# The first stage's projection as three fp32r passes, with statistics a quarter ahead, two load buffers and the normalisation on ScalarE

## The reference

```
x = x + ssm(layernorm(x))      # depthwise conv of 4 taps, projection 512 -> 48, a scan over 2048 steps, 16 -> 512
x = x + moe(layernorm(x))      # router over 64 experts, top 8, expert FFNs 512 -> 256 -> 512, and a shared expert
```

## Time and profile before

| what | value |
|---|---|
| median of 3 runs | 3797.72 us (3794.5 to 3801.96) |
| the profiled execution | 3804.61 us |
| its span | 3802.9 us |
| TensorE busy over the span | 3527.6 us, 93% |
| VectorE, ScalarE, GpSimd busy | 2331.9, 1363.0, 1736.2 us |
| granted TensorE clock over the span | 0.972 of full |
| `ssm_inputs`, TensorE's first transpose to its last matmul | 31.52 to 197.9 us |

### The profile page before, as it was taken

How to read it: one execution, slowest core, us unless ns; L and a number is a source line. 1 busy time by engine, 2 the same in 40 slices (tenths; PEclk the granted TensorE clock), 3 DMA queues, 4 the chain that set the end, 5 groups by cost and what they waited for, 6 DMA issues and landing times.

```text
span 3802.9 us, 109938 instructions
## 1 busy us (share of the span) xinstructions
PE 3527.6 (93%) x17240; PEld 2860.7 (75%) x17241; DVE 2331.9 (61%) x5877; ACT 1363.0 (36%) x4103; POOL 1736.2 (46%) x1372
## 2 busy tenths in 40 slices
PE   5929999589999999999999999999999999999995
PEld 3518888378787888787888788888887878888884
DVE  5457888555656666566555656665565666656552
ACT  2224444133334333343333433333333334333331
POOL 1011212145555555555555555555555555555543
PEclk9969999789999999999999999999999999999998
DMA  3323333256767666676667666666666677667654
GB/s 126 105 80 124 119 128 115 52 130 122 159 141 166 148 135 140 142 172 139 140 111 159 157 131 123 142 142 142 127 140 125 139 174 157 139 127 170 128 99 72
DMA packets 217551, 502.59 MB, mean 132 GB/s; under 512 B 47504, under 2 KB 47632, under 8 KB 217114
## 3 DMA queue, kind: packets, MB, share of 16 engines
q0 software_dynamic: 129024, 320.94, 45.4%
q1 hardware_dynamic: 87130, 176.22, 13.8%
q10 hardware_dynamic: 1344, 4.85, 0.4%
HBM read 1115.79 MB, written 191.41 MB: 344 GB/s over the span
## 4 chain that ended last, share of the span: by engine, by line
PE 73%; issue 3%; DMA 2%; DVE 1%; DVEq 1%; ACT 1%; ACTq 0%; POOLq 0%; POOL 0%; SPq 0%
PE e_ps_gu L1597 41%; PE e_ps_y L1616 20%; PE e_ps_x L1567 7%; PE e_ps_h L1626 3%; DMA out<-e_y,e_y_ids 2%; PE e_ps_find L1579 1%; DVE e_w_low L1738 1%; DVEq L1451 0%; ACT e_w_high L1675 0%; DVE e_below L1781 0%; ACT e_xT_high L1683 0%; DVEq L1741 0%; ACTq L1451 0%; DVE e_xT_low L1746 0%; DVEq L1738 0%
## 5 line engine op out<-in xcount | busy, mean ns | idle before, releaser
L1531 POOL DMA_INDIRECT out<-e_y,e_y_ids x576 | 992.7, 1723 | 1237.1 <-SPq L1501 600.9
L1597 PE MATMUL e_ps_gu<-e_w_high,e_xT_high 128*128 x2304 | 687.6, 419 | 32.8 <-issue 27.3
L1523 POOL DMA_INDIRECT e_x<-token_rows,e_x_ids x576 | 618.4, 1074 | 214.3 <-issue 169.9
L1597 PE MATMUL e_ps_gu<-e_w_high,e_xT_low 128*128 x2304 | 636.7, 398 | 0.0
L1597 PE MATMUL e_ps_gu<-e_w_low,e_xT_high 128*128 x2304 | 635.2, 398 | 0.0
L1694 ACT ACTIVATE e_silu<-e_ps_gu 128x256 f32<-128x256 f32 x576 | 221.3, 384 | 1018.1 <-PE e_ps_gu L1597 839.4
L1765 DVE TENSOR_SCALAR e_y<-e_ps_y,e_weight 128x512 f32 (+1 forms) x576 | 430.4, 747 | 235.9 <-PE e_ps_y L1616 196.8
L1746 DVE TENSOR_TENSOR e_xT_low<-e_ps_x,e_xT_high 128x512 fp32r<-128x512 f32 x576 | 397.5, 690 | 269.6 <-ACT e_xT_high L1683 123.0
L1597 PEld LDWEIGHTS e_ps_gu<-e_w_high,e_xT_low 128*128 128x128 f32 x2304 | 436.4, 189 | 107.3
L1597 PEld LDWEIGHTS e_ps_gu<-e_w_low,e_xT_high 128*128 128x128 f32 x2304 | 434.6, 189 | 102.4
L1597 PEld LDWEIGHTS e_ps_gu<-e_w_high,e_xT_high 128*128 128x128 f32 x2304 | 396.0, 191 | 113.2 <-issue 51.1
(11 more groups left out here) (292 smaller groups left out, 4141.5 us busy)
## 6 DMA issues: line engine op xcount, KB each, us to landing
e_w_raw<-in_L_ffn_we_gate SPq DMA_DIRECT2D x576, 512.0 KB
e_w_raw<-in_L_ffn_we_up SPq DMA_DIRECT2D x576, 512.0 KB
e_w_raw<-in_L_ffn_we_down SPq DMA_DIRECT2D x576, 512.0 KB
a_x<-in_L_attn_x SPq DMA_DIRECT2D x64, 256.0 KB, 3.6
t_x_in<-in_L_attn_x SPq DMA_DIRECT2D x64, 256.0 KB, 2.7
token_rows<-t_xn SPq DMA_DIRECT2D x64, 256.0 KB, 2.0
out<-t_y_out SPq DMA_DIRECT2D x64, 256.0 KB, 2.0
e_x<-token_rows,e_x_ids POOLq DMA_INDIRECT x576
```

The lines of the kernel that those rows point to most:

```text
L1523: pool.indirect_dma_start(x[:, s % XS, :], None, k.rows, bass.IndirectOffsetOnAxis(x_ids[:, s:s + 1], 0)) \
L1531: pool.indirect_dma_start(k.out, bass.IndirectOffsetOnAxis(y_ids[:, s:s + 1], 0), y[:, s % YS, :], None, compute_op=ALU.add).then_inc(adde ...
L1597: last = nc.tensor.matmul(ps_gu[s % 2][:], x[:, s % 2, c, :], w[:, c], start=(n == 0), stop=(n == 3 * DC - 1))
```

## The change

- The product becomes three passes in fp32r: `a_wtap_high` and `a_wtap_low` are made once; the turned block is kept as `a_xT_high` (ScalarE, `keep_high`) and `a_xT_low` (VectorE, `keep_low`: turned minus high). A quarter's product is 24 matmuls of 128x512 in place of 8 fp32 ones.
- TensorE's order: the product of quarter n - 1 is cut in four parts of six matmuls, and one part follows each transposed block of quarter n.
- VectorE takes the statistics of quarter n + 1 before the subtractions of quarter n, and computes `a_shift` = -mean * rstd behind them. It no longer normalises.
- ScalarE normalises (`normalize`: x * rstd + shift), a block ahead of the high copies. The stores of a batch (`store`) follow the batch's last product, which is now finished in the next batch's first quarter.
- `a_x` has two buffers of four blocks. `a_xT_low` lies in memory (`shared_rows`) that `scan_states` later uses for the states and the output weights.

```diff
-        x_in = sb("a_x", [P, SUB, D])
+        x_in = sb("a_x", [P, 2, SUB, D])
         stats = sb("a_stats", [P, SUB, 6])
         moments = sb("a_moments", [P, SUB, 2])
         var_eps = sb("a_var_eps", [P, SUB])
-        rstd = sb("a_rstd", [P, SUB])
+        rstd = sb("a_rstd", [P, 2, SUB])
+        shift = sb("a_shift", [P, 2, SUB])
         xn = sb("a_xn", [P, SUB, D])
-        xnT = sb("a_xnT", [P, DC, L + 2])
+        xT_high = sb("a_xT_high", [P, DC, L + 2], F32R)
+        xT_low = k.shared_rows[:].rearrange("p (c l) -> p c l", c=DC)
...
+        wtap_high = sb("a_wtap_high", [P, 2, DC, P], F32R)
+        wtap_low = sb("a_wtap_low", [P, 2, DC, P], F32R)
...
-                        sp.wait_ge(normed, NT * b + SUB * q + s + 1)
-                        sp.dma_start(x_in[:, s, :], k.x_blocks[b, SUB * q + s]).then_inc(x_loaded[s], 16)
+                        after(sp, normed, SUB * (n - 2) + s + 1)
+                        sp.dma_start(x_in[:, q % 2, s, :], k.x_blocks[b, SUB * q + s]).then_inc(x_loaded[q % 2][s], 16)
...
+            nc.vector.tensor_copy(wtap_high[:], wtap[:])
+            v.drain()
+            nc.vector.tensor_tensor(wtap_low[:], wtap[:], wtap_high[:].bitcast(F32), ALU.subtract)
             v.drain().then_inc(w_ready, 1)
+            def spread(b, q):
+                half, load = q % 2, 2 * b + q // 2
+                for s in range(SUB):
+                    v.wait_ge(x_loaded[half][s], 16 * load + 16)
+                    nc.vector.bn_stats(stats[:, s, :], x_in[:, half, s, :])
+                v.drain()
+                for s in range(SUB):
+                    nc.vector.bn_aggr(moments[:, s, :], stats[:, s, :])
+                v.drain()
+                nc.vector.tensor_scalar(var_eps[:], moments[:, :, 1], LN_EPS, None, ALU.add).then_inc(var_ready, 1)
+
+            def shifts(b, q):
+                v.wait_ge(rstd_ready, QT * b + q + 1)
+                nc.vector.scalar_tensor_tensor(out=shift[:, q % 2], in0=moments[:, :, 0], scalar=-1.0,
+                                               in1=rstd[:, q % 2], op0=ALU.mult, op1=ALU.mult).then_inc(shift_ready, 1)
+
+            def keep_low(b, q, s):
+                i = SUB * (QT * b + q) + s
+                v.wait_ge(xT_high_ready, i + 1)
+                after(v, product_done, QT * b + min(q + 2, QT) - QT)
+                at = 1 + P * (SUB * q + s)
+                nc.vector.tensor_tensor(xT_low[:, :, at:at + P], turned[s][:], xT_high[:, :, at:at + P].bitcast(F32),
+                                        ALU.subtract).then_inc(xT_low_ready, 1)
+
+            def batch(b):
+                for q in range(QT):
+                    next_b, next_q = (b, q + 1) if q + 1 < QT else (b + 1, 0)
+                    more = not isinstance(next_b, int) or next_b < B
+                    if more:
+                        spread(next_b, next_q)
+                    for s in range(SUB):
+                        keep_low(b, q, s)
+                    if more:
+                        shifts(next_b, next_q)
+
+            spread(0, 0)
+            shifts(0, 0)
             v.wait_ge(bias_summed, 1)
             nc.vector.tensor_tensor(bias[0:PROJ, :], bias_ps[0:PROJ, :], b48[:], ALU.add).then_inc(bias_ready, 1)
-
-            with v.Fori(0, B * QT) as n:
-                for s in range(SUB):
-                    v.wait_ge(x_loaded[s], 16 * n + 16)
-                    nc.vector.bn_stats(stats[:, s, :], x_in[:, s, :])
-                v.drain()
-                for s in range(SUB):
-                    nc.vector.bn_aggr(moments[:, s, :], stats[:, s, :])
-                v.drain()
-                nc.vector.tensor_scalar(var_eps[:], moments[:, :, 1], LN_EPS, None, ALU.add).then_inc(var_ready, 1)
-                v.wait_ge(rstd_ready, n + 1)
-                for s in range(SUB):
-                    v.wait_ge(turned_done, SUB * n + s + 1)
-                    nc.vector.tensor_scalar(xn[:, s, :], x_in[:, s, :], moments[:, s, 0:1], rstd[:, s:s + 1],
-                                            ALU.subtract, ALU.mult).then_inc(normed, 1)
+            peeled(v, B, batch)
...
+            def turn(b, q, s):
+                i = SUB * (QT * b + q) + s
+                pe.wait_ge(normed, i + 1)
+                after(pe, xT_low_ready, i + 1 - SUB)
+                for c in range(DC):
+                    last = nc.tensor.transpose(turned[s][:, c, :], xn[:, s, c * P:(c + 1) * P], k.ident[:])
+                last.then_inc(turned_done, 1)
+
+            def project(b, q, part):
+                n = QT * b + q
+                pair, first = part // 2, 6 * (part % 2)
+                if part == 0:
+                    pe.wait_ge(xT_low_ready, SUB * (n + 1))
+                    after(pe, proj_ready, n - 1)
+                if part == 2 and q + 1 < QT:
+                    pe.wait_ge(xT_low_ready, SUB * (n + 1) + 1)
+                at = QL * q + 2 * pair
+                passes = [(x, w, c) for x, w in ((xT_high, wtap_high), (xT_high, wtap_low), (xT_low, wtap_high))
+                          for c in range(DC)]
+                for j in range(first, first + 6):
+                    x, w, c = passes[j]
+                    last = nc.tensor.matmul(product[q % 2][:], w[:, pair, c, :], x[:, c, at:at + QL],
+                                            start=(part == 0 and j == 0), stop=(part == 3 and j == 11))
+                if part == 3:
+                    last.then_inc(product_done, 1)
+
+            def batch(b):
+                for q in range(QT):
+                    last_b, last_q = (b, q - 1) if q > 0 else (b - 1, QT - 1)
+                    for s in range(SUB):
+                        turn(b, q, s)
+                        if not isinstance(last_b, int) or last_b >= 0:
+                            project(last_b, last_q, s)
+
+            peeled(pe, B, batch)
+            for part in range(4):
+                project(B - 1, QT - 1, part)
...
+            def normalize(b, q, s):
+                n = QT * b + q
+                if s == 0:
+                    act.wait_ge(shift_ready, n + 1)
+                after(act, turned_done, SUB * (n - 1) + s + 1)
+                nc.scalar.activation(xn[:, s, :], x_in[:, q % 2, s, :], ACT.Identity, bias=shift[:, q % 2, s:s + 1],
+                                     scale=rstd[:, q % 2, s:s + 1]).then_inc(normed, 1)
+
+            def keep_high(b, q, s):
+                act.wait_ge(turned_done, SUB * (QT * b + q) + s + 1)
+                after(act, product_done, QT * b + min(q + 2, QT) - QT)
+                at = 1 + P * (SUB * q + s)
+                nc.scalar.copy(xT_high[:, :, at:at + P], turned[s][:]).then_inc(xT_high_ready, 1)
...
-                act.wait_ge(product_done, QT * b + q + 1 + QT)
+                act.wait_ge(product_done, QT * b + q + 1)
...
+            def store(b):
                 nc.scalar.copy(proj[0:PROJ, L - 1:L], b48[:]).then_inc(last_set, 1)
...
+            def batch(b):
+                for q in range(QT):
+                    normalize(b, q, 0)
+                    for s in range(1, SUB):
+                        normalize(b, q, s)
+                        keep_high(b, q, s - 1)
+                    keep_high(b, q, SUB - 1)
+                    if q > 0:
+                        keep_product(b, q - 1)
+                    elif not isinstance(b, int) or b > 0:
+                        keep_product(b - 1, QT - 1)
+                        store(b - 1)
+
             peeled(act, B, batch)
+            keep_product(B - 1, QT - 1)
+            store(B - 1)
...
-            k.wout_high = sb("wout_high", [P, B, D], F32R)
-            k.wout_low = sb("wout_low", [P, B, D], F32R)
-            k.states = sb("states", [P, 2, L], F32R)
+            k.shared_rows = sb("shared_rows", [P, DC * (L + 2)], F32R)
+            k.states = k.shared_rows[:, 0:2 * L].rearrange("p (c l) -> p c l", c=2)
+            k.wout_high, k.wout_low = (k.shared_rows[:, at:at + B * D].rearrange("p (b d) -> p b d", b=B)
+                                       for at in (2 * L, 2 * L + B * D))
```

More of the change, by code:

```diff
@@ L181, in ssm_inputs @@
         w_loaded = sem("w_loaded")
-        x_loaded = [sem(f"x_loaded{i}") for i in range(SUB)]
-        dve = sem("dve")
+        x_loaded = [[sem(f"x_loaded{i}{s}") for s in range(SUB)] for i in range(2)]
         w_ready = sem("w_ready")
@@ L193, in ssm_inputs @@
         turned_done = sem("turned_done")
-        xnT_ready = sem("xnT_ready")
+        shift_ready = sem("shift_ready")
+        xT_high_ready = sem("xT_high_ready")
+        xT_low_ready = sem("xT_low_ready")
         product_done = sem("product_done")
@@ L224, in _ @@
         def _(pool):
-            def quarter(n):
-                pool.wait_ge(var_ready, n + 1)
-                nc.gpsimd.tensor_tensor(rstd[:], var_eps[:], k.nhalf[:], ALU.pow).then_inc(rstd_ready, 1)
-            with pool.Fori(0, B * QT) as n:
-                quarter(n)
+            with pool.Fori(0, B * QT // 2) as n:
+                for half in range(2):
```

(40 more changed lines are left out.)

18 lines of the change are left out of this document (4 added, 14 removed).

## The result

The changed kernel takes 3803.47 us (median of 22 executions) where the kernel before takes 3797.11 (22, the same chip). The ratio is 1.0016, 95% interval 1.001 to 1.0022, so by the ratio it is 6.1 us longer, 3.8 to 8.4: clear of zero, and in the middle less than the 0.2% (7.6 us) that was set as the bound of no change, which the upper end passes. Two of the 22 executions, 5858 and 19457 us, were disturbed and are not in the ratio. The profiled execution of the changed kernel is its shortest, 3798.70 us (span 3797.0), while that of the kernel before is a long one. What the changed one leads by, it gains behind the stage: from the experts' first search (`e_ps_find`) to the span's end it takes 3032.0 us, and 3041.5 before. So the stage is compared by its own end, and the whole by the ratios.

The account below looks back on a forecast made before the run. TensorE was taken to bound the stage. Start 40.7, work 112.8, ordinary waits 18.2, store waits 18.8, last product 5.8 and clock 6.9 sum to 203.2 us, 5.3 over 197.9; median 3797.7 + 5.3 = 3803, range 3794 to 3819.

Parts of the forecast that it names:

- last product: TensorE's final product after the 15 quarters: 24 matmuls of 0.235 plus 0.16, 5.8 us.
- The work of a quarter: TensorE's transposes, switches and 24 fp32r matmuls at 0.235 each: 7.52 us a quarter, against 8.61 before.
- The ordinary wait: TensorE idle at a quarter's end until ScalarE normalises the next first block: 1.65 us, 11 times, 18.2.
- All four pieces: Serial parts of the ordinary wait: ScalarE's start 0.20, product copy 0.59, normalisation 0.81, TensorE's start 0.05 us.
- The second-chain rival: Low copy and shift later than their 0.4 us slack; late by 1 us, total +13.7, 3811; chance 0.33.
- The store waits: TensorE idle at three batch ends while ScalarE issues stores: 6.05 us each, once 6.7, together 18.8.
- The start: Weights split, statistics, first normalisation at 33.5, then quarter 1's transposes starting at 40.7 us.
- The clock: Slow TensorE clock behind the three store waits, 2.0 us each, and 0.9 at the start: 6.9 us.
- The place on ScalarE: Normalisation takes 0.81 us on ScalarE against 0.545 on VectorE; in 14 waits this costs 3.7 us.
- The loads: Buffers are freed a quarter earlier than needed, so waits for loads vanish, at no gain since they were hidden.

Follow-up runs that it names:

- e1: Changed kernel with ScalarE's normalisation of the next quarter's first block put ahead of the product copy; ratio 0.9981 to the kernel before.
- e2: e1 with VectorE's shift also computed after the second subtraction, not the fourth; ratio 0.9949 to the kernel before.
- e7: Changed kernel with only VectorE's shift moved behind the second subtraction; ratio 1.0011 to the kernel before.
- e5: The changed kernel run again unaltered, on another chip; ratio 1.0018 to the kernel before.
- e4: Kernel before, with only the output weights and states moved into the shared allocation `shared_rows`; ratio 1.0003 to the kernel before.
- e3: e2 with each batch's six stores issued by SyncE behind the third quarter's loads, not by ScalarE; ratio 0.9921 to the kernel before.
- e8: Kernel before, with only the six stores of a batch issued by SyncE behind quarter 1's loads; ratio 0.9985 to the kernel before.

## Why the prediction was right

The forecast was 3803.0, the measured median 3803.47, and the mechanism is the one summed: TensorE's work shrinks, and a serial wait at every quarter's end and longer waits behind the stores give it back. That the two figures agree within 0.5 us is luck: the stage was forecast 5.3 longer and is 3.6 longer in its trace, the ratio says 6.1 with an interval of 3.8 to 8.4, and the terms miss to both sides. Term by term, from the changed kernel's trace:

| term | forecast | measured (brackets) |
|---|---|---|
| quarter 1's transposes start | 40.7 | 42.5 |
| 15 quarters of TensorE work | 7.52 each, 112.8 | 7.52 each, 112.8 |
| 11 ordinary waits | 1.65 each, 18.2 | 1.53 each, 16.9 |
| 3 store waits | 18.8 | 16.1 |
| last product | 5.8 | 5.8 |
| clock | 6.9 | 7.5 (the rest) |
| last matmul ends | 203.2 | 201.5 |

The prediction took both work and waits by starts. Counted so, the trace has 7.34 of work a quarter (110.1), ordinary waits of 1.66 to 1.82 (1.71 in the mean, 18.8) and 16.6 at the stores. Against these the forecast has 2.7 too much work, 0.6 too little ordinary wait, 2.2 too much at the stores, 1.8 too little in the start and 0.6 too little for the clock: 1.9 too much in all (1.7 by the last line; the rest is rounding).

- **The work of a quarter** is 0.18 shorter than forecast; that 7.52 stands in both columns is chance. The first part takes 1.88 (52.90 to 54.78), as summed. The other three take 1.81 to 1.83, since in them four transposes take 0.35 and not 0.39, and a group of four 0.91 and not 0.94. Four fp32r matmuls take 0.91 to 0.94 (197.67 to 198.58, 198.58 to 199.52), so one takes 0.23. The Trainium skill ("FP8 and Floating Point Precision", TensorE Precision Notes) has true fp32 as four passes, which makes 0.214 an estimate for one from our 0.858; the trace doesn't reach it: 0.228 in the fastest stretch of four. The prediction's "both later groups" of `token_tiles` have 0.235 is right of the one that the earlier trace rows show; the third stands behind two more transposes and takes 1.02.
- **The ordinary wait.** All four pieces are there in series: at 103.47 ScalarE starts, 0.2 after TensorE is through by starts, the copy holds it to 104.05, the normalisation of 0.81 ends at 104.86, TensorE starts at 104.98. e1 shows that taking the product copy out of them takes only 0.5 off, since the shift comes next; with the shift earlier too, e2 leaves about 0.25. The second-chain rival, held at 0.33, was not at work here (e7). It limits e1: by the ratios e1 gains 13 us on the changed kernel, e7 2 (within the noise), both together 25.
- **The store waits** were mis-sized, 16.1 for 18.8: the six issues take 3.2 us here and took 3.7 at the place that was read (the row below, from the kernel before), and from the product copy to the next ACTIVATE it is 4.52 in place of 4.98.

```profile
76.50 3.71 ACTq L353 DMA_DIRECT2D ssm_proj<-a_proj  x6
```

- **The start** went in the other direction, 1.8 late. One microsecond of it is none of the change: VectorE's first work on the weights waits for a load, until 21.78 before and until 22.91 here (22.25 to 23.05 in the ten experiments). The split of the weights was priced about right: the statistics begin 5.7 behind that point, 5.8 by the forecast. The other 0.8 lies between the first normalisation (34.47) and quarter 1's transposes, where ScalarE waits 0.50 and 0.60 for transposes. The earlier shift of e7 gives 1.1 of start back (41.39), but the forecast had the shift behind the last subtraction as well. VectorE before and after, then ScalarE and TensorE after:

```profile
21.78 0.20 DVE L241 COPY a_win<-a_win 128x64 f32<-128x64 f32 x1 [8.67 <-DMA a_b_pair<-in_L_attn_b_in]
```

```profile
22.91 0.20 DVE L244 COPY a_win<-a_win 128x64 f32<-128x64 f32 x1 [9.83 <-DMA a_b_pair<-in_L_attn_b_in]
...
40.17 0.59 ACT L373 CAST a_xT_high<-a_turned 128x512 fp32r<-128x512 f32 x1 [0.60 <-PE a_turned L318]
...
43.22 2.06 PE L334 MATMUL a_product<-a_xT_high,a_wtap_high 128*128 128x512 f32 x4
45.08 0.85 PE L334 MATMUL a_product<-a_xT_high,a_wtap_low 128*128 128x512 f32 x2
```

- **The clock** fell in mid-stage behind the three store waits alone, and its price there was 2.7, 1.8 and 1.4 (84.01 to 95.91 is 11.90, less 7.52 and the wait of 1.64), 6.0 together as forecast. The prediction's argument that a longer gap can't cost less is not borne out: the gap of 5.20 us cost 1.4, one of 4.02 before 1.8. In the start it is 1.4, where four matmuls take 1.86 (43.22 to 45.08) against 1.01 later, although the granted clock of that stretch (42.5 to 45) reads 1.00; so that this term is the clock is not shown.
- **The place on ScalarE** (3.7 us for 0.81 against 0.545) was not tried by itself. The rule in the Trainium skill ("ScalarE: Activation LUTs", Rules for kernel authors) would have the normalisation on VectorE; e2's order leaves it on ScalarE, and a quarter's end waits for it only the hidden 0.25 us. Most of the price was that of the place in the stream; what the engine adds is open.
- **The loads** cost nothing, as said: VectorE has no wait for `a_x` in the changed kernel.

What stays open: the stage explains 3.6 us (4.6 in e5) of 6.1 (6.8), and 1.1 of that is the later arrival of the weights. The intervals begin at 3.8 and 3.4. Nothing behind the stage is longer in the traces: stage end to the experts' first search is 563.5 us in both kernels, and from there to the span's end it is 3041.5 before, 3032.0 and 3031.8 (e5) changed, 3039.6 in e4. Over the table the two columns differ by -3.9 to +6.1, to both sides, and this last stretch alone varies by more than the missing 2.5. Where those are is not shown.

Where the gain went is shown, then. Against the kernel before, by the brackets, TensorE's work is 17.6 us shorter over the stage, the ordinary waits are 16.9, the stores take 3.4 more (16.1 for the 4.02, 4.66 and 4.01 before), quarter 1's transposes start 2.2 later (42.46 for 40.27), and the slow stretches cost 1.2 less: 3.7 longer in all.

## What to carry to other kernels

When work is moved to another engine, write down that engine's stream at the place where the bounding engine waits, and look at what stands ahead of the instruction it waits for: here a copy of 0.59 us and six DMA issues of 3.2 us that nobody was waiting for. Two steps moved (one on ScalarE, one on VectorE) turned a change that lost 6 us into one that gained 19; the first alone gained 7 and the second alone nothing that shows, so after taking one chain away look for the next one and its slack. A DMA issue moved off a busy engine goes into another stream, where a wait ahead of it holds everything behind. Putting it behind the loads that will be wanted during that wait worked in the new order (e3); in the old one it wasn't tried. And a bracket is counted from a modelled end: check a row without one by the distance of starts.

## What the runs showed that I had not expected

- A second load buffer made the old kernel no faster that shows (stage -4.1 against -7.4, ratios 0.9979 and 0.9985 with overlapping intervals): SyncE arrives earlier at its waits for the product, 89.9 us in place of 44.9.
- The clock outlasts the gap for a while: in e2, TensorE is idle for 3.1 us up to 79.22, the four transposes behind it run at full pace (79.22 to 79.62), and from 80.5 the granted clock is 0.50. Windows of e2:

```profile
76.00:79.20 3.20, 0.09 (x1) 0.00 (x0) 0.85 (x6) 0.93 (x2) 1.01 (x1) 1.00 0.89 231
80.50:83.00 2.50, 2.50 (x10) 2.02 (x9) 0.76 (x2) 1.24 (x3) 0.00 (x0) 0.50 0.80 211
```

  So a shorter gap (3.1 us for 5.5) did not save the clock, nor did 2.58 us in e8 (0.55 from 89 to 91); in e3, without such gaps, it stands at 1.00 from 45 to 160.
- Four fp32 transposes followed by an fp32 product cost more than followed by an fp32r one in the same place (0.49 and 0.41 us behind a wait, 0.43 and 0.35 in mid-quarter).
